# Order of the first transfers of a two-layer transformer kernel: x of the first pair first, the other x behind the small loads, columns and positions on ACT's queue

## The reference

```
# layer 0
ada = silu(cond) @ Wada.T + bada        # gamma1, gamma2, scale1, scale2, shift1, shift2
x = x + attn0(ln(x)*(scale1+1)+shift1) * gamma1     # 16 heads of 16, q and k normalised
x = x + (gelu((ln(x)*(scale2+1)+shift2) @ Wfc1.T + bfc1) @ Wfc2.T + bfc2) * gamma2
# layer 1
x = x + attn1(rms(x) * ln1_w*(1 + cond @ tw1.T)) @ Wo.T   # 8 query heads of 32, one kv head, rope(pos)
h = rms(x) * ln2_w*(1 + cond @ tw2.T)
x = x + (silu(h @ Wg.T) * (h @ Wu.T)) @ Wd.T
```

## Time and profile before

| what | value |
|---|---|
| median of three runs | 309.8 us (308.78 to 311.77) |
| the profiled execution | 313.7 us, of which 311.6 us span from its first to its last instruction |
| mean granted clock of TensorE | 0.967 of full |
| busy share of the span | PE 93%, DVE 69%, ACT 66%, POOL 49% |
| transfers | 14.28 MB, mean 46 GB/s; nearly all in the first sixth |

### The profile page before, as it was taken

The page is one execution under the profiler, slowest core; times in us unless marked ns, Lnnn a source line. Parts: engine busy times, 40 slices in busy tenths (PEclk is TensorE's granted clock), DMA queues, the critical chain, the costliest instruction groups (busy, mean ns, idle before and its releaser), DMA issues.

```text
span 311.6 us, 7095 instructions
## 1 busy us (share of the span) xinstructions
PE 291.3 (93%) x2412; PEld 244.5 (78%) x2412; DVE 215.4 (69%) x527; ACT 205.5 (66%) x698; POOL 153.9 (49%) x289
## 2 busy tenths in 40 slices
PE   7999979898879989978999999999999999999996
PEld 7879767666757768865987787899888988888985
DVE  4884599979496999988859787576445875463431
ACT  3574399999975998987889865737772342662210
POOL 3658687385976955797424456521424321222000
PEclk9795899999986999999999999999999999999999
DMA  6999532002010010000002000000000000000000
GB/s 185 243 299 331 150 104 97 8 1 70 0 36 0 16 54 3 1 3 0 2 0 69 1 3 0 2 2 17 18 3 2 0 8 28 1 2 25 12 2 34
DMA packets 14035, 14.28 MB, mean 46 GB/s; under 512 B 1568, under 2 KB 12960, under 8 KB 14000
## 3 DMA queue, kind: packets, MB, share of 16 engines
q1 hardware_dynamic: 14000, 13.83, 14.7%
HBM read 12.76 MB, written 1.06 MB: 44 GB/s over the span
## 4 chain that ended last, share of the span: by engine, by line
PE 56%; DVE 19%; POOL 12%; issue 6%; ACT 4%; DMA 1%; SPq 1%; DVEq 0%; POOLq 0%
PE ps_shared L1570 16%; PE ps_shared L1377 8%; PE ps_shared L1379 7%; PE ps_shared L1378 7%; PE ps_shared L1543 4%; DVE z L1265 3%; PE ps_output L1524 2%; PE ps_shared L1508 2%; ACT z L990 2%; PE ps_scores L1497 2%; DVE neg_max L1276 2%; PE ps_scores L1407 2%; PE ps_shared L1413 2%; DMA X<-in_x 1%; PE ps_shared L1397 1%
## 5 line engine op out<-in xcount | busy, mean ns | idle before, releaser
L990 ACT ACTIVATE z<-z,neg_max 128x128 f32<-128x128 f32 x128 | 49.9, 404 | 5.8 <-DVE neg_max L1276 5.8
L830 POOL TENSOR_TENSOR h_lo<-xn,h_hi 128x256 fp32r<-128x256 f32 x32 | 24.1, 756 | 35.5 <-ACT h_hi L954 31.6
L1570 PE MATMUL ps_shared<-Wfc2T,g_h 128*128 128x256 f32 x128 | 33.0, 403 | 0.5 <-DVE g_h L1335 0.5
L1508 PE MATMUL ps_shared<-ident,z 128*128 128x128 f32 x192 | 29.4, 276 | 4.1 <-ACT z L990 1.9
L994 ACT ACTIVATE z<-ps_scores,neg_max 128x128 f32<-128x128 f32 x64 | 22.6, 368 | 14.7 <-DVE neg_max L1282 14.4
L1010 ACT ACTIVATE probsT<-ps_shared 128x512 f32<-128x512 f32 x48 | 28.8, 599 | 4.6 <-PE ps_shared L1508 3.6
L884 POOL TENSOR_TENSOR z<-z,row_inv 128x512 f32<-128x512 f32 x16 | 16.6, 1040 | 28.7 <-DVE row_inv L1290 28.5
L1570 PE MATMUL ps_shared<-WdT,g_h 128*128 128x256 f32 x128 | 30.1, 381 | 0.5 <-DVE g_h L1348 0.5
L1046 ACT ACTIVATE g_a<-ps_shared 128x256 f32<-128x256 f32 x32 | 12.4, 386 | 25.8 <-PE ps_shared L1379 21.4
L1508 PEld LDWEIGHTS ps_shared<-ident,z 128*128 128x128 f32 x192 | 22.0, 140 | 8.7 <-issue 6.3
L1570 PEld LDWEIGHTS ps_shared<-Wfc2T,g_h 128*128 128x128 f32 x128 | 24.2, 199 | 5.0 <-issue 1.0
(11 more groups left out here) (164 smaller groups left out, 884.7 us busy)
## 6 DMA issues: line engine op xcount, KB each, us to landing
gamma<-gamma_scratch SPq DMA_DIRECT2D x8, 256.0 KB, 3.6
stage<-in_Wada SPq DMA_DIRECT2D x6, 256.0 KB, 4.9
X<-in_x SPq DMA_DIRECT2D x4, 256.0 KB, 3.8
stage<-in_Wqkv SPq DMA_DIRECT2D x4, 256.0 KB, 5.5
Wfc2T<-in_Wfc SPq DMA_DIRECT2D x1, 1024.0 KB, 8.1
stage<-in_Wfc SPq DMA_DIRECT2D x4, 256.0 KB, 5.2
WdT<-in_Wd SPq DMA_DIRECT2D x1, 1024.0 KB, 6.7
stage<-in_Wg SPq DMA_DIRECT2D x4, 256.0 KB, 2.6
```

The source lines that it names most:

```text
L830: pool.tensor_tensor(h_lo[:, m, :, j * P:(j + 1) * P], h_full[:, m, j, :, :], h_hi[:, m, :, j * P:(j + 1) * P].bitcast(F32), ALU.subtract) ...
L990: ins = act.activation(z[:, d, u, :], z[:, d, u, :], ACT.Exp, bias=neg_max[:, d, u:u + 1], accum_out=head_sum[:, n % 2, t, u, b:b + 1])
L1508: ins = pe.transpose(bank[:, u * P:(u + 1) * P], z[:, G % DEEP, u, :], ident[:, :])
L1570: ins = pe.matmul(psum[b][:, 0:C], g_h[:, f, j * P:(j + 1) * P], WT1[name][:, f, :], start=(f == 0), stop=(f == FT - 1))
```

## The change

Only the order and the queue of the first transfers change. The list of SP is rewritten after the simulation: `load_x(0)`, the five staging chunks, the seven small loads, and then `load_x(1)`, `load_x(2)`, `load_x(3)`. Everything behind them keeps its order. The transfers of the columns and positions are issued by ACT, ahead of its first step, instead of by SP. The lists of PE, DVE, ACT's steps and POOL stay as they are, and no wait is added or taken away.

```diff
 ORDER, PLAN, PLANNED_US = make_orders()
+FIRST = ([("load_x", 0)] + [("load", c) for c in range(STAGE)] + [("load_small",)]
+         + [("load_x", p) for p in range(1, PAIRS)])
+ORDER["SP"] = FIRST + [k for k in ORDER["SP"] if k not in FIRST]
...
-            sp.dma_start(cols[:, 2 * N_SEQ:V0 + N_VEC], columns).then_inc(vec_loaded, 16)
-            sp.dma_start(pos_i[:, :], pos).then_inc(pos_loaded, 16)
...
         @block.scalar
         def _(act):
+            act.dma_start(cols[:, 2 * N_SEQ:V0 + N_VEC], columns).then_inc(vec_loaded, 16)
+            act.dma_start(pos_i[:, :], pos).then_inc(pos_loaded, 16)
```

## The result

The changed kernel takes 314.99 us (median of 4 runs, 314.52 to 317.1) against 310.5 us for the kernel before (median of 4, 308.78 to 311.77): ratio 1.0156, interval 1.0119 to 1.0193. It is slower, by 4.5 us between the medians. The profiled execution took 314.52 us with a span of 312.6 us. Both kernels issue the same seven small loads; in the listing of the queue before, under "The change", the last of them (`res_bias<-in_bfc`, issued at 8.70 us in the trace) is missing.

The account below looks back on a forecast made before the run. TensorE, busy 93%, was taken as bound, its start hanging on VectorE. Pair 1's wait of 3.7 us plus 0.6 of clock gave 4.3, added to the median 309.8: 314.1 us, range 308.8 to 318.2.

Parts of the forecast that it names:

- Two issues and two X leave the place ahead of the chunks.: Kernel start: chunks issued 1.9 us earlier; first statistics gain at most 1.1 us, modulation at most 0.7.
- Columns and positions on ACT.: Kernel start: angles end between 6.2 and 7.1 us, giving back up to 0.9; hidden, so no cost on the path.
- Pair 1 behind the small loads.: VectorE's third statistics row waits for pair 1, landing at 13.2 us; first product 3.7 us later, ends 2.7 and 4.5.
- the sum by stages: Pair 1's landing estimated by adding stage times for pair 0, chunks, then small loads and one X: 12.2 us, lower end.
- The upper end, by the issue: Pair 1's landing estimated from its place in the queue being issued 1.9 us earlier: 14.0 us.
- Clock.: TensorE stands from about 10 to 14.5 us, then half clock near the first product: 0.6 us, ends 0 and 2.4.
- The half-clock stretch from 23.37 to 33.60.: TensorE's later slow stretch moves with the work: 0 us, ends -5.1 (all at full) and +1.7 (a third longer).
- rival C: Not slower: the later start shrinks the half-clock stretch of 10.23 us, all at full saving 5.1; 308.4 us, chance 0.12.
- B: At the start, pair 1 lands soon after its issue, at 10.1 us, costing 0.6 us; 310.4 us, chance 0.07.
- D: Clock lost as well: both products at half (2.4 us), later stretch a third longer (1.7); 317.6 us, chance 0.11.
- E: Delay partly absorbed where TensorE is busy only 3.71 of 5 us, from 35 to 40; 311.9 us if half, chance 0.10.
- The first term: The sum's 3.7 us for VectorE's third statistics row, and so the first product, waiting for pair 1.

Follow-up runs that it names:

- e7: Changed kernel with x of pair 1 right behind pair 0, and rotary angles and sines later in VectorE's and ACT's lists: 309.03 against 309.58 us, ratio 0.9983.
- e3: Kernel before with only columns and positions issued by ACT, x in the old order: 310.06 us, ratio 0.9986.
- e1: Changed kernel with x of pair 1 moved right behind x of pair 0, ahead of the chunks: 309.35 against 310.13 us for the kernel before, ratio 0.9981.
- e4: Kernel before with only x of pair 1 moved behind the small loads, columns and positions still on SP: 315.89 us, ratio 1.0183.
- e2: Changed kernel, transfers untouched, pair 1's statistics and roots later in VectorE's and GpSimd's lists: 311.12 against 310.13 us for the kernel before, ratio 1.0026.
- second profiles: Both kernels profiled again, unchanged: before 308.96 us (span 306.9), after 314.92 us (span 312.9).
- e5: Changed kernel with four small bias loads reading 128 different weight rows instead of one row 128 times: 311.69 against 309.58 us for the kernel before, ratio 1.004.

## Why the prediction was right, and where its terms were off

The forecast was 314.1 us, 4.3 above the median of 309.8 that stood for the kernel before; measured were 314.99, 4.5 above its median of 310.5 in the comparison. Slower by over 1% had been given 0.64, and that came.

- *Two issues and two X leave the place ahead of the chunks.* Right. The last chunk landed 3 us earlier. The gain came to nothing, as worked out: VectorE's angles were late next, and 3.3 us of earlier statistics in e7 showed that they had been. One bound broke without a consequence: modulation started 1.4 us earlier (6.49 against 7.88) and not at most 0.7, as the warm-ups took 5.14 us and not 5.66.
- *Columns and positions on ACT.* Right, hidden. e3 puts the part at a ratio of 0.9986, its interval around 1, and its first statistics at 7.41 (7.22 in the change, neither with a wait) show the angles ending just behind the estimate's 7.1.
- *Pair 1 behind the small loads.* Right in mechanism and place: e1, e4 and e2 show it from three sides. The size was off: 3.7 us was taken, with ends of 2.7 and 4.5, and 5.3 (14.85 - 9.58) and, between the second profiles, 5.0 (14.40 - 9.40) were measured, both above the upper end. The step that failed is the sum by stages, in which the small loads with one X behind them took 4.75 us, as they had before. They took 14.85 - 8.14 = 6.7 us. The upper end, by the issue, failed too, since pair 1 needed 7.9 us from issue to landing and not pair 2's 6.7. e5 gives what the four broadcast loads cost, 3.4 us of landing, but this does not explain the miss, since their slowness was in the 4.75 us too. Why the same seven loads and one X took 6.7 us behind the last chunk here and 4.75 before is open: the chunks came 3 us earlier, the x behind the small loads only 1.0 (14.8 against 15.9). The second profiles repeat it, with 5.8 us (8.54 to 14.38) and 4.3 us (10.92 to 15.25), and the slow windows move less in the change (76, 68 and 69 GB/s from 9 to 12 us) than before (99 and 89 from 11 to 13).
- *Clock.* TensorE stood from 10.27 to 16.12, and the level was at half behind it, as expected. The 0.6 us was a guess between 0 and 2.4. In the first profile the first product ran at full (0.23 us a matmul at once), in the second at 0.50 until 20.7 us, which costs 1.0 us. So the lower end occurred, and 1.0 of the upper end's 2.4; both products at half occurred in neither. The fall itself came in the stand in both profiles (and in e4's, at half from 11.2 to 21.4 us); how far behind the product's start it lasts has no single value.
- *The half-clock stretch from 23.37 to 33.60.* It is not in every execution: the second profile of before does not have it. Where it occurs it does stand at one place of the work, as the text had it: in six of the 13 profiles a stretch at half starts 9.6 to 11.6 us behind the first product, 9.6 in the first profile of before (23.37) and 10.1 in that of the change (29.1, there only 3.4 us long). What makes it come or not is open. The profiled execution that the sum was made against, 313.7 us, was slower than all of the other runs of its kernel; its two later stretches are 4.5 of the 4.7 us by which it is behind the second profile. Taking the difference to the median off, which the text did, kept it out of the forecast. The price of rival C, -5.1 us for the whole stretch, was too large: the stretch cost 2.3 us. The text itself had named POOL, busy 9.39 of 10.23 us there, as what would bound next; that this is the reason was not tested.
- *Rivals.* B (pair 1 soon after its issue) fell: pair 1 needed 7.9 us. The page "DMA: Bandwidth & Descriptors" of the Trainium skill, section "Anatomy of one DMA", has a rule for GpSimd's path, from which the estimate is 2.6 us for one transfer of this size. The trace agrees with it for pair 0, which was issued first with nothing ahead of it and needed 2.9 us, and not for pair 1. C did not come: the later stretch was indeed shorter in the first profile of the change (3.4 us) and missing in the second, but the time came out slower all the same. D came in part: in the second profile the stand brought 1.0 us of half clock at the product, and one of the four runs took 317.1 us, at the lowest mean clock. E, absorption, fell: between the second profiles the 6.0 us by which TensorE is behind at 24 us are undiminished at the end.

So the direction and the mechanism were right by reasoning, and the closeness of the total (0.9 us, and 0.2 as a difference) was in part luck. The first term was too small by 1.3 to 1.6 us, the clock term of 0.6 was 0 in one profile and 1.0 in the other, and the two pairs of profiles differ in span by 1.0 and 6.0 us where the medians differ by 4.5. How the stretches at half clock were spread over the runs behind the medians was not traced.

## What to carry to other kernels

A transfer's place in a queue is to be read against the list of the engine that waits for it: here the second pair's data were not urgent, but the instruction that wanted them stood ahead of the first pair's work on an engine that runs in order, and moving the transfer (e1) mends all of it, moving the instruction (e2) some 3.5 of 4.5 us. Price what stands ahead in a queue by kind, not by bytes: seven small loads with 0.6 MB, four of them broadcasts of one row to 128 partitions, and one x took 6.7 us to land behind the chunks, where the five chunks with 1.25 MB took 4.5 us behind pair 0. And look at one kernel's clock in more than one profile before a stretch at half clock is given a cause in the program.

## What the runs showed of the hardware that was not expected

Four loads of 128 KB that each read one 1 KB row 128 times left the DMA engines busy (0.78 to 1.12) at 68 to 76 GB/s; from 128 different rows the same stretch moved 259 to 308 GB/s. A second profile of an unchanged kernel had 1.00 of the clock over its whole span where the first had three stretches at half (mean 0.967), worth 4.7 us of 311.6. The first of these stretches at half cost 0.2 us, the second 2.3 us in 10.2. And with the slow loads on ACT's queue both queues moved data in the same 2 us (0.43 and 0.27 MB), while a transfer of SP's queue that was issued before them landed 1.4 us later than with the slow loads behind it on its own queue (10.2 against 8.7).
